# Routed expert layer on one core: fixed row blocks for each expert's first 128 rows, another block order, and twelve constant matmuls behind the ranks

## The chip, the cores and the metric

The program runs on one core of a Trainium2 chip. The metric is the device time of one execution in microseconds. Names of engines: PE is TensorE (PEld its weight loads), DVE is VectorE, ACT is ScalarE, POOL is GpSimd, SP is SyncE, which here only issues DMAs. L12 is line 12 of the kernel.

## The reference

The input x has 1024 rows of 128 values (D). A layer of attention over a context of 6404 rows comes first, then the part that is changed here: a layer of eight experts, of which each row uses one.

```
x = x + cross_attention(layernorm(x), ctx)
xn = layernorm(x)
expert_id = argmax(xn @ wr + br)                 # 8 experts
h = gelu(xn @ w1[e] + b1[e])                     # 128 -> 512
y = h @ w2[e] + b2[e]                            # 512 -> 128
out = x + y of the row's own expert
```

## The kernel before

**Tiles.** The 1024 rows are eight tiles of 128. The attention fills the first 172 us of the span. The last of its tiles is late, so the eighth tile takes no part in the sorting of rows by expert: all eight experts are run over it and a mask keeps the right one. These are the eight **dense** blocks. The other seven tiles (TA = 7) are **sent**: each row goes to a place in a table in HBM, sorted by expert, and the table is read back in 14 blocks of 128 rows (NB), one expert to a block. A block that no row fell into is computed as well. There are 22 blocks in all. `DENSE_AT` names the eight places in the order of 22 at which a dense block stands, `SENT_AT` the other fourteen.

**From the router to the table.** PE computes router scores, DVE takes the best expert of each row as a one-hot table (`oneh`), PE turns that into `rank_psum` (a row's number within its expert) and `count_psum` (rows per expert), L1216 to L1223. DVE then computes where each row goes, in a chain in which every instruction waits for the one ahead of it (`link`): blocks per expert (`nblk`), start of each expert (`sblk`), row position (`pos`), L947 to L957. The expert of each block (`bexp`) follows at L961 to L968. POOL sends the seven tiles with one indirect DMA each (L602). SP waits for all seven (`rows_sent`) and reads the blocks back in four batches of 3, 4, 4 and 3 (`block_rows`, L449), first the normalised rows, then the rest (`rest_landed`).

**Weights.** `wp` holds the weights of all experts, 512 columns to each. Which expert a sent block belongs to is known only at run time, so SP copies its 512 KB from `wp` into a slot of `PT` or `qn` (`fetch`, L444), 14 copies, with two ahead of the wait for `rows_sent`. Dense blocks read `wp` in place.

**A block on the engines.** PE's `up(b)` is 16 matmuls (L1276 to L1279), ACT applies GELU twice (L710, L711), DVE takes the low half (L985), PE's `down(b)` is 9 matmuls (L1290 to L1296), DVE finishes the block in two halves (L995 and L1011 for a sent block, L1001 and L1014 for a dense one). PE issues `up` two blocks ahead of `down`. The eighth tile comes to PE through a transpose at L1227, for which DVE normalises it at L762. Sent rows come to PE through `turn(g)`, the transposes of a batch (L1245), which ACT (L700) and DVE (L977) bring back to SBUF. On PE, `turn(0)` stands just ahead of `up` of the first sent block, and two dense `down`s stand behind that `up`. POOL writes each finished sent block to the output by an indirect DMA (L608); the last dense block's result is written by SP (L476).

Of the kernel before, what the change touches and what calls it, by code (L numbers as in the profile page):

```python
# [30 lines left out]
P = 128  # L31


def build(nc, x, ctxT, w3, b3, wlT, b_l, wr, br, w1, b1, w2, b2, out):
# [47 lines left out]
    with es:  # L82
        def sb(name, shape, dt=F32):
            return es.enter_context(nc.sbuf_tensor(name, shape, dt))

        def sem(name):
            return es.enter_context(nc.semaphore(name))

        tri = sb("tri", [P, E, E])
# [52 lines left out]
        kedge = sb("kedge", [P, E, TA])  # L142
        slot_no = sb("slot_no", [P, NB, E])
# [7 lines left out]
        ints = stageT[:, XRE - NB * E:XRE].bitcast(I32)  # L151
# [17 lines left out]
        more = carve(E * TA).rearrange("p (a b) -> p a b", b=TA)  # L169
        below = carve(E * E).rearrange("p (a b) -> p a b", b=E)  # L170
        rank = carve(TA * E).rearrange("p (a b) -> p a b", b=E)
        cand = carve(T * E).rearrange("p (a b) -> p a b", b=E)
        mask = carve(E)
        chosen = carve(NB // 2, F16)
        past = carve(NB * E).rearrange("p (a b) -> p a b", b=E)
        oneh = carve(TA * E // 2, F16).rearrange("p (a b) -> p a b", b=E)
        nblk, sblk, eblk = carve(E), carve(E), carve(E)
        posf, rmx, bexpf = carve(TA), carve(T), carve(NB)
        pos, bexp = carve(TA, I32), carve(NB, I32)
# [93 lines left out]
        block_w_landed = [sem(f"block_w_landed{k}") for k in range(WSLOTS)]  # L273
# [87 lines left out]
        def block_w(b):  # L361

            k = b % WSLOTS
            return spare[k // (WSLOTS // 2)][:, k % (WSLOTS // 2) * 4 * F:(k % (WSLOTS // 2) + 1) * 4 * F]\
                .rearrange("p (a f) -> p a f", f=F)

        @block.sync
        def _(sp):
# [65 lines left out]
            expert_reg = [sp.alloc_register(f"expert{j}") for j in range(NB)]  # L434
            sp.wait_ge(w_low, T)
            sp.wait_ge(experts_ready, 1)
            sp.reg_load(expert_reg[0:FIRST], bexp[0:1, 0:FIRST])
            ex = [sp.snap(r, min_val=0, max_val=E - 1) for r in expert_reg[0:FIRST]]
# [12 lines left out]

            for b in range(FIRST):
                fetch(b)
            sp.reg_load(expert_reg[FIRST:NB], bexp[0:1, FIRST:NB])
            ex += [sp.snap(r, min_val=0, max_val=E - 1) for r in expert_reg[FIRST:NB]]
# [4 lines left out]
            block_rows(0, D, ROW, rest_landed)  # L460
            fetch(3)
            block_rows(1, D, ROW, rest_landed)
            fetch(4)
            fetch(5)
            block_rows(2, 0, D, rows_landed)
            fetch(6)
            block_rows(2, D, ROW, rest_landed)
            fetch(7)
            fetch(8)
            block_rows(3, 0, D, rows_landed)  # L470
            fetch(9)
            block_rows(3, D, ROW, rest_landed)
            for b in range(10, NB):
                fetch(b)
# [5 lines left out]
        def _(pool):  # L480
# [29 lines left out]
            def numbers(dst, n, pattern, base=0):  # L510
# [4 lines left out]
            numbers(kedge[:, :, :].rearrange("p e k -> p (e k)"), E * TA, [[0, E], [P, TA]])  # L515
            numbers(slot_no[:, :, :].rearrange("p b e -> p (b e)"), NB * E, [[P, NB], [0, E]])
            then(nc.gpsimd.memset(tri[:, :, :], float(P)))
            then(nc.gpsimd.affine_select(out=tri[:, :, :], in_=tri[:, :, :], compare_op=ALU.is_gt, fill=0.0, base=0,
                                         pattern=[[1, E], [-1, E]], channel_multiplier=0))
            then(nc.gpsimd.memset(ones16[:, :], 1.0))  # L520
# [199 lines left out]
        def _(dve):  # L720
# [204 lines left out]
            def best(logits, t0, t1):  # L925
# [23 lines left out]
            link(nc.vector.tensor_reduce(out=nblk[:, :], in_=more[:, :, :], axis=AX.X, op=ALU.add))  # L949
            link(nc.vector.tensor_tensor(below[:, :, :], tri[:, :, :],  # L950
                                         nblk[:, :].unsqueeze(1).broadcast_to([P, E, E]), ALU.mult))
            link(nc.vector.tensor_reduce(out=sblk[:, :], in_=below[:, :, :], axis=AX.X, op=ALU.add))
            link(nc.vector.tensor_tensor(rank[:, :, :], rank_psum.rearrange("p (t e) -> p t e", e=E),
                                         sblk[:, :].unsqueeze(1).broadcast_to([P, TA, E]), ALU.add))
# [6 lines left out]
            link(nc.vector.scalar_tensor_tensor(out=eblk[:, :], in0=nblk[:, :], scalar=float(P), in1=sblk[:, :],  # L961
                                                op0=ALU.mult, op1=ALU.add))
            link(nc.vector.tensor_tensor(past[:, :, :], eblk[:, :].unsqueeze(1).broadcast_to([P, NB, E]),
# [70 lines left out]
        def _(pe):  # L1034
# [190 lines left out]

            pe.wait_ge(x2n_ready, H + 1)
# [21 lines left out]
            def weights(b):  # L1248

                if b in SENT_AT:  # L1250
                    return block_w(SENT_AT.index(b))
                k = DENSE_AT.index(b)
                return wp[:, :, k * F:(k + 1) * F]

            def bias_rows(b):

                if b in SENT_AT:
                    return chosen[:, SENT_AT.index(b):SENT_AT.index(b) + 1].broadcast_to([P, P])
                return pick[:, DENSE_AT.index(b), :]
# [89 lines left out]
```

## Time and profile before

| | |
|---|---|
| time, median of 3 runs | 234.27 us (232.66 to 235.13) |
| the profiled execution's own time | 234.39 us |
| its span, first to last instruction | 232.7 us |
| busy share of the span: PE, DVE, ACT, POOL | 86%, 78%, 68%, 55% |
| mean granted TensorE clock | 0.944 |
| matmuls on PE, instructions on DVE | 1837, 395 |

The shares are means over two stages with different limits, the attention and the experts. The change lies in the second, which begins at about 172 us, so the views below are cut to stretches of time. The granted clock is 1.00 at 2.4 GHz and 0.50 at 1.2 GHz. The span is 1.69 us shorter than the execution's own time.

### The profile page before, as it was taken

What the parts mean: (1) busy time and instruction counts of PE and PEld (TensorE: products, weight loads), DVE (VectorE), ACT (ScalarE), POOL (GpSimd) and SP (SyncE); (2) the same over time, 40 slices, a digit from 0 to 9 for tenths busy, and PEclk for the clock granted to TensorE, in tenths of its full rate; (3) what the DMA queues carried; (4) which work ended last, traced back from release to release, by engine and by line L of the source; (5) the groups of instructions that cost most, each with busy time, mean ns of one, the idle gap of its engine ahead of it and who ended that gap; (6) DMA issues with size and microseconds to landing.
All of it is one profiled execution on the core that took longest, in us unless ns stands there. A gap on an engine that the chain in (4) does not pass through costs nothing.

```text
span 232.7 us, 5011 instructions
## 1 busy us (share of the span) xinstructions
PE 201.1 (86%) x1837; PEld 150.3 (65%) x1837; DVE 180.6 (78%) x395; ACT 157.9 (68%) x249; POOL 128.6 (55%) x177
## 2 busy tenths in 40 slices
PE   0379969999999999989989899899993797999980
PEld 0133417776766767757666566789973686899970
DVE  2899797697998998998995997958756435776872
ACT  2752899399399699699595799689531445667650
POOL 3695718807915807978508947744400740066763
PEclk9999985899999999999999999999996569999998
DMA  6999979899999999999999999988994369999200
GB/s 215 389 251 263 226 223 237 192 234 174 220 215 216 278 230 269 241 198 233 216 213 256 184 220 258 201 196 185 239 263 121 120 219 290 346 370 378 98 11 12
DMA packets 142958, 51.78 MB, mean 223 GB/s; under 512 B 121172, under 2 KB 140773, under 8 KB 142934
## 3 DMA queue, kind: packets, MB, share of 16 engines
q1 hardware_dynamic: 142000, 50.08, 93.2%
q0 software_dynamic: 784, 1.38, 1.7%
q8 instruction: 14, 0.23, 0.4%
q14 instruction: 10, 0.08, 0.1%
q10 hardware_dynamic: 150, 0.00, 0.0%
HBM read 10.74 MB, written 3.75 MB: 62 GB/s over the span
## 4 chain that ended last, share of the span: by engine, by line
PE 49%; DVE 21%; DMA 11%; issue 8%; ACT 4%; POOL 3%; SPq 2%; DVEq 0%; POOLq 0%
DMA PT<-Phl 10%; PE psX L1079 5%; PE psS L1061 5%; PE psO L1079 5%; PE psS L1060 5%; PE psS L1059 5%; DVE S L800 5%; DVE Phl L817 3%; PE psS L1290 3%; PE psX L1081 3%; PE psO L1081 3%; ACT S L651 3%; SPq L393 2%; PE psS L1276 2%; PE psS L1296 2%
## 5 line engine op out<-in xcount | busy, mean ns | idle before, releaser
L651 ACT ACTIVATE S<-S,negb 128x1024 f32<-128x1024 f32 x48 | 55.1, 1147 | 18.4 <-DVE negb L808 18.4
L800 DVE TENSOR_SCALAR_CACHE_REDUCE S<-psS 128x1024 f32<-128x1024 f32 x48 | 58.2, 1217 | 11.4 <-PE psS L1061 11.2
L817 DVE TENSOR_TENSOR Phl<-S,Phl 128x1024 f16<-128x1024 f32 x38 | 51.5, 1355 | 5.0 <-ACT Phl L666 4.8
L533 POOL TENSOR_TENSOR Phl<-S,Phl 128x256 f16<-128x256 f32 x40 | 26.3, 689 | 51.7 <-ACT Phl L666 51.7
L666 ACT CAST Phl<-S 128x1024 f16<-128x1024 f32 x48 | 50.3, 1047 | 5.2 <-DMA PT<-Phl 3.7
L1059 PE MATMUL psS<-qT,gh 128*128 128x512 f16 x96 | 37.7, 393 | 5.4 <-DVE S L800 2.6
L1079 PE MATMUL psX<-qn,PT 128*128 128x256 f16 x204 | 36.4, 273 | 2.1 <-DMA PT<-Phl 2.1
L1079 PE MATMUL psO<-qn,PT 128*128 128x256 f16 x204 | 37.3, 276 | 0.9 <-DMA PT<-Phl 0.8
L1061 PE MATMUL psS<-qT,gl 128*128 128x512 f16 x96 | 37.9, 395 | 0.0
L1060 PE MATMUL psS<-qT,gh 128*128 128x512 f16 x96 | 37.9, 394 | 0.0
L1081 PE MATMUL psO<-qn,PT 128*128 128x128 f16 x204 | 35.7, 221 | 0.0
L1081 PE MATMUL psX<-qn,PT 128*128 128x128 f16 x204 | 35.0, 219 | 0.0
L608 POOL DMA_INDIRECT out_x<-stageT,S x14 | 17.7, 1265 | 22.1 <-DVE stageT L1011 17.1
L1079 PEld LDWEIGHTS psX<-qn,PT 128*128 128x128 f16 x204 | 20.0, 98 | 7.5 <-DMA PT<-Phl 3.5
L1079 PEld LDWEIGHTS psO<-qn,PT 128*128 128x128 f16 x204 | 20.3, 99 | 6.3 <-DMA PT<-Phl 1.9
L710 ACT ACTIVATE Phl<-psS 128x512 f16<-128x512 f32 x22 | 13.2, 598 | 15.4 <-PE psS L1279 9.0
L1081 PEld LDWEIGHTS psO<-qn,PT 128*128 128x128 f16 x204 | 20.2, 99 | 2.2 <-issue 0.3
L1081 PEld LDWEIGHTS psX<-qn,PT 128*128 128x128 f16 x204 | 20.0, 98 | 1.9
L1059 PEld LDWEIGHTS psS<-qT,gh 128*128 128x128 f16 x96 | 9.8, 102 | 14.6 <-DVE S L800 3.5
L1061 PEld LDWEIGHTS psS<-qT,gl 128*128 128x128 f16 x96 | 9.7, 101 | 12.1 <-issue 1.4
L985 DVE TENSOR_TENSOR Phl<-Phl 128x512 f16<-128x512 f32 x22 | 15.0, 682 | 2.4 <-issue 2.4
L574 POOL TENSOR_TENSOR wp<-wp 128x256 f16<-128x256 f32 x16 | 15.6, 1005 | 0.3
(239 smaller groups left out, 425.3 us busy)
## 6 DMA issues: line engine op xcount, KB each, us to landing
PT<-wp SPq DMA_DIRECT2D x8, 512.0 KB, 6.0
stageT<-in_ctxT SPq DMA_DIRECT2D x6, 512.0 KB, 7.0
qn<-wp SPq DMA_DIRECT2D x6, 512.0 KB, 7.3
wp<-in_w SPq DMA_DIRECT2D x4, 512.0 KB, 4.9
stageT<-in_w SPq DMA_DIRECT2D x4, 512.0 KB, 4.9
rows_by_expert<-stageT SPq DMA_DIRECT2D x4, 385.5 KB, 5.6
PT<-Phl SPq DMA_TRANSPOSE x48, 4.2
S<-rows_by_expert SPq DMA_DIRECT2D x2, 258.0 KB, 5.4
```

The costliest lines, as they stand in the source:

```text
L533: last = nc.gpsimd.tensor_tensor(lo[:, r], slot(t, e)[:, r], hi[:, r], ALU.subtract)
L574: last = nc.gpsimd.tensor_tensor(parts[:, 1, at + a:at + a + CHUNK], src[:, a:a + CHUNK], parts[:, 0, at + a:at + a + CHUNK], ALU.subtract)
L608: pool.indirect_dma_start(out=out, out_offset=bass.IndirectOffsetOnAxis(ap=rows[:, b, 2 * D:ROW].bitcast(I32), axis=0), in_=yf[:, b, :], i ...
L651: nc.scalar.activation(slot(t, e), slot(t, e), ACT.Exp, bias=negb[:, t:t + 1], accum_out=Lp[:, t * NG + e:t * NG + e + 1]).then_inc(exp_do ...
L666: nc.scalar.copy(hi, slot(t, e)).then_inc(high_done, 1)
L800: nc.vector.tensor_scalar(out=into, in0=bank(u, n)[:, 0:into.shape[1]], scalar1=1.0 / GS, scalar2=None, op0=ALU.mult, op1=ALU.max, accum_o ...
L817: nc.vector.tensor_tensor(lo, slot(t, e), hi, ALU.subtract).then_inc(low_done, 1)
L1059: nc.tensor.matmul(dst, g_h, hi, start=True, stop=False)
L1060: nc.tensor.matmul(dst, g_h, lo, start=False, stop=False)
L1061: last = nc.tensor.matmul(dst, g_l, hi, start=False, stop=True)
L1079: nc.tensor.matmul(acc[:, 0:2 * D].rearrange("p (a d) -> p a d", a=2), PT[:, 2 * e * TW + i, :], both[:, :, i, :], start=(j == 0), stop=Fa ...
L1081: last = nc.tensor.matmul(acc[:, 0:D], PT[:, 2 * e * TW + n + i, :], both[:, 0, i, :], start=False, stop=(j == QT - 1), skip_group_check=True)
```

## The change

The table of 14 blocks stays, but its blocks have another meaning. Blocks 0 to 7 belong to experts 0 to 7 and take each expert's first 128 rows. Blocks 8 to 13 (NX = 6 of them) take rows past the first 128 of any expert, and only their expert is found at run time. So eight of the fourteen sent blocks read their weights in `wp` in place, with constant bias rows (`pick`), and six are copied by `fetch`. SP issues no copy ahead of `rows_sent` any more.

The position is now computed by expert times 128, plus rank, plus a shift if the rank is 128 or more: two more instructions in the chain on DVE, and a copy of a constant ahead of it. POOL makes one more column of a table of constants (two small instructions in the attention's time). `DENSE_AT` becomes six dense blocks first, fourteen sent, two dense last. PE computes twelve matmuls of 512 columns on constants (`fill`) between the ranks and the transpose at L1227; nothing reads their result.

```diff
-    NB = TA + E - 1
+    NX = TA - 1
+    NB = E + NX
-    DENSE_AT = (0, 1, 2, 3, 4, 10, 16, 21)
+    DENSE_AT = (0, 1, 2, 3, 4, 5, 20, 21)
-    ROUTE_CONSTS = 19
-    WSLOTS = 12
-    FIRST = 2
+    ROUTE_CONSTS = 21
...
-            def fetch(b):
-
-                if b >= WSLOTS:
-                    sp.wait_ge(y_in_psum, SENT_AT[b - WSLOTS] + 1)
-                sp.dma_start(block_w(b), wp[:, :, bass.ds(ex[b] * F, F)]).then_inc(block_w_landed[b % WSLOTS], 16)
+            def fetch(k):
+
+                sp.dma_start(block_w(k), wp[:, :, bass.ds(ex[k] * F, F)]).then_inc(block_w_landed[k], 16)
...
-            for b in range(FIRST):
-                fetch(b)
...
             sp.wait_ge(rows_sent, 16 * TA)
             block_rows(0, 0, D, rows_landed)
             block_rows(1, 0, D, rows_landed)
+            block_rows(0, D, ROW, rest_landed)
+            block_rows(1, D, ROW, rest_landed)
+            block_rows(2, 0, D, rows_landed)
+            fetch(0)
+            block_rows(2, D, ROW, rest_landed)
+            fetch(1)
+            block_rows(3, 0, D, rows_landed)
             fetch(2)
...
-            numbers(slot_no[:, :, :].rearrange("p b e -> p (b e)"), NB * E, [[P, NB], [0, E]])
...
+            numbers(slot_no[:, :, :].rearrange("p b e -> p (b e)"), NX * E, [[P, NX], [-P, E]], base=(E - 1) * P)
...
+            numbers(tri[:, :, E], E, [[-P, E]], base=(E - 1) * P)
...
+            link(nc.vector.tensor_copy(extra[:, E:E + 1], ones[:, 0:1]))
             dve.wait_ge(ranks_in_psum, 1)
-            link(nc.vector.tensor_tensor(more[:, :, :], count_psum.unsqueeze(2).broadcast_to([P, E, TA]),
+            link(nc.vector.tensor_tensor(more[:, :, :], count_psum.unsqueeze(2).broadcast_to([P, E, NX]),
                                          kedge[:, :, :], ALU.is_gt))
...
-            link(nc.vector.tensor_tensor(rank[:, :, :], rank_psum.rearrange("p (t e) -> p t e", e=E),
-                                         sblk[:, :].unsqueeze(1).broadcast_to([P, TA, E]), ALU.add))
+            link(nc.vector.tensor_reduce(out=shift[:, :], in_=below[:, :, :], axis=AX.X, op=ALU.add))
+            ranks = rank_psum.rearrange("p (t e) -> p t e", e=E)
+            link(nc.vector.scalar_tensor_tensor(out=over[:, :, :], in0=ranks, scalar=float(P),
+                                                in1=shift[:, :].unsqueeze(1).broadcast_to([P, TA, E]),
+                                                op0=ALU.is_ge, op1=ALU.mult))
+            link(nc.vector.scalar_tensor_tensor(out=rank[:, :, :], in0=iob.broadcast_to([P, TA, E]), scalar=float(P),
+                                                in1=ranks, op0=ALU.mult, op1=ALU.add))
+            link(nc.vector.tensor_tensor(rank[:, :, :], rank[:, :, :], over[:, :, :], ALU.add))
...
+            filler = ones[:, :].bitcast(F16)
+
+            def fill(n):
+
+                for _ in range(n):
+                    nc.tensor.matmul(psS[2][:, 0:CH], filler[:, 0:P],
+                                     filler.unsqueeze(1).broadcast_to([P, 2, 2 * P]), start=True, stop=True)
+
+            fill(12)
+
             pe.wait_ge(x2n_ready, H + 1)
             nc.tensor.transpose(x7T_psum, x2n[:, TA, :], idf[:, :]).then_inc(x7T_in_psum, 1)
...
             def weights(b):
 
-                if b in SENT_AT:
-                    return block_w(SENT_AT.index(b))
-                k = DENSE_AT.index(b)
-                return wp[:, :, k * F:(k + 1) * F]
+                j = SENT_AT.index(b) if b in SENT_AT else DENSE_AT.index(b)
+                return wp[:, :, j * F:(j + 1) * F] if j < E else block_w(j - E)
...
                     pe.wait_ge(xT_low, g + 1)
-                    pe.wait_ge(block_w_landed[j % WSLOTS], 16 * (j // WSLOTS + 1))
-                    pe.wait_ge(chosen_rows, 1)
+                    if j >= E:
+                        pe.wait_ge(block_w_landed[j - E], 16)
+                        pe.wait_ge(chosen_rows, 1)
```

The order of instructions is written out by hand, so the diff moves them at three places. The first is DVE's chain from the ranks to the positions. Before (S holds the small tables of the router; kedge and tri are tables of constants):

```order
L737 BN_AGGR mv<-st 128x2 [waits dve_chain]
L947 TENSOR_TENSOR S<-psS,kedge 128x56 [waits ranks_in_psum,dve_chain]
L949 TENSOR_REDUCE S<-S 128x8 [waits dve_chain]
L950 TENSOR_TENSOR S<-tri,S 128x64 [waits dve_chain]
L952 TENSOR_REDUCE S<-S 128x8 [waits dve_chain]
L953 TENSOR_TENSOR S<-psS,S 128x56 [waits dve_chain]
L955 TENSOR_TENSOR S<-S 128x56 [waits dve_chain]
L956 TENSOR_REDUCE S<-S 128x7 [waits dve_chain]
L957 CAST S<-S 128x7 [waits dve_chain]
```

Now, the same place on DVE:

```order
L726 BN_AGGR mv<-st 128x2 [waits dve_chain]
L935 COPY S<-ones 128x1 [waits dve_chain]
L937 TENSOR_TENSOR S<-psS,kedge 128x48 [waits ranks_in_psum,dve_chain]
L939 TENSOR_REDUCE S<-S 128x8 [waits dve_chain]
L940 TENSOR_TENSOR S<-tri,S 128x72 [waits dve_chain]
L942 TENSOR_REDUCE S<-S 128x8 [waits dve_chain]
L944 SCALAR_TENSOR_TENSOR S<-psS,S 128x56 [waits dve_chain]
L947 SCALAR_TENSOR_TENSOR S<-iota_e,psS 128x56 [waits dve_chain]
L949 TENSOR_TENSOR S<-S 128x56 [waits dve_chain]
L950 TENSOR_TENSOR S<-S 128x56 [waits dve_chain]
L951 TENSOR_REDUCE S<-S 128x7 [waits dve_chain]
L952 CAST S<-S 128x7 [waits dve_chain]
```

The copy and two instructions on 128x56 are new; the rest of the chain is as long as it was.

The second place is PE between the ranks and the first dense block. Before:

```order
L1223 MATMUL psS<-S,ones 128x8 x7
L1227 MATMUL psO<-idf,qT 128x128 [waits x2n_ready]
L1276 MATMUL psS<-S,wp 128x128 [waits w_low,x7T_low,route_consts,b12_ready]
L1277 MATMUL psS<-S,wp 128x128
L1278 MATMUL psS<-S,wp 128x128
```

Now, on PE:

```order
L1218 MATMUL psS<-S,ones 128x8 x7
L1226 MATMUL psS<-ones 128x512 x12
L1232 MATMUL psO<-idf,qT 128x128 [waits x2n_ready]
L1279 MATMUL psS<-S,wp 128x128 [waits w_low,x7T_low,route_consts,b12_ready]
L1280 MATMUL psS<-S,wp 128x128
```

The twelve matmuls wait for nothing but stand ahead of the transpose of the eighth tile.

The third place is SP's queue behind the filling of the empty table (ISA is a register instruction ahead of a copy). Before:

```order
L437 TENSOR_LOAD S [waits experts_ready,w_low]
L438 ISA
L444 DMA PT<-wp 128x4x512
L444 ISA
L444 DMA PT<-wp 128x4x512
L454 TENSOR_LOAD S
L455 ISA x2
L449 DMA S<-rows_by_expert 128x3x128 [waits rows_sent]
L449 DMA S<-rows_by_expert 128x4x128
L444 ISA
L444 DMA PT<-wp 128x4x512
L449 DMA S<-rows_by_expert 128x3x129
```

Now, on SP:

```order
L436 TENSOR_LOAD S [waits experts_ready,w_low]
L437 ISA
L446 DMA S<-rows_by_expert 128x3x128 [waits rows_sent]
L446 DMA S<-rows_by_expert 128x4x128
L446 DMA S<-rows_by_expert 128x3x129
L446 DMA S<-rows_by_expert 128x4x129
L446 DMA S<-rows_by_expert 128x4x128
L441 ISA
L441 DMA PT<-wp 128x4x512
```

The two copies of weights that stood ahead of the row reads are gone, and five row reads stand ahead of the first copy.

## Rows read from the trace of the kernel before

**Rows 1.** Stretches: us, busy of PE, PEld, DVE, ACT, POOL, granted clock, DMA share, GB/s.

```profile
182.40:189.00 6.60, 6.60 (x55) 6.25 (x56) 1.99 (x10) 2.32 (x5) 5.08 (x6) 0.50 0.69 245
189.00:190.00 1.00, 1.00 (x12) 0.88 (x11) 0.00 (x0) 0.00 (x0) 0.47 (x1) 0.68 0.26 95
...
193.60:195.43 1.83, 0.56 (x4) 0.32 (x4) 1.73 (x4) 1.13 (x3) 0.00 (x0) 1.00 1.05 344
...
195.43:227.63 32.20, 30.91 (x454) 29.07 (x454) 21.60 (x57) 20.20 (x38) 16.33 (x13) 1.00 0.72 240
```

**Rows 2.** PE in order of time, 176 to 196 us: start, us, line, idle before.

```profile
176.96 0.33 PE L1223 MATMUL psS<-S,ones 128*128 128x8 f16 x7
181.07 0.48 PE L1227 MATMUL psO<-idf,qT 128*128 128x128 f32 x1 [3.78 <-DVE qT L762]
182.39 0.27 PE L1276 MATMUL psS<-S,wp 128*128 128x128 f16 x1 [0.84 <-DVE S L966]
...
185.16 0.27 PE L1276 MATMUL psS<-S,wp 128*128 128x128 f16 x1
...
193.72 0.55 PE L1245 MATMUL psX<-idf,S 128*128 128x128 f32 x3
195.43 0.23 PE L1276 MATMUL psS<-S,PT 128*128 128x128 f16 x1 [1.16 <-DVE S L977]
```

**Rows 3.** DVE in order of time, 177 to 229 us.

```profile
177.44 0.22 DVE L947 TENSOR_TENSOR S<-psS,kedge 128x56 f32<-128x56 f32 x1
...
179.20 0.17 DVE L957 CAST S<-S 128x7 int32<-128x7 f32 x1
...
180.67 0.35 DVE L762 TENSOR_SCALAR qT<-qT,mv,rstd 128x128 f32<-128x128 f32 x1
...
185.41 0.69 DVE L985 TENSOR_TENSOR Phl<-Phl 128x512 f16<-128x512 f32 x1 [2.38 <-issue]
...
225.71 0.28 DVE L1011 TENSOR_TENSOR stageT<-psS,stageT 128x128 f32<-128x128 f32 x1
...
228.12 0.35 DVE L1014 SCALAR_TENSOR_TENSOR stageT<-psS,S,stageT 128x128 f32<-128x128 f32 x1
```

**Rows 4.** POOL in order of time, 35 to 229 us.

```profile
35.66 2.56 POOL L533 TENSOR_TENSOR Phl<-S,Phl 128x256 f16<-128x256 f32 x4 [5.58 <-ACT Phl L666]
...
185.60 1.33 POOL L602 DMA_INDIRECT rows_by_expert<-qT,S  x1 [0.30 <-issue]
187.24 0.96 POOL L602 DMA_INDIRECT rows_by_expert<-qT,S  x1 [0.30 <-issue]
...
228.33 0.98 POOL L608 DMA_INDIRECT out_x<-stageT,S  x1 [0.31 <-issue]
```

**Rows 5.** SP's DMA issues in order of time, 183 to 192 us.

```profile
183.90 1.50 SPq L444 DMA_DIRECT2D PT<-wp  x2
191.11 0.90 SPq L449 DMA_DIRECT2D S<-rows_by_expert  x2
```

**Rows 6.** PE in order of time, 201 to 204 us, two sent blocks.

```profile
201.39 0.23 PE L1276 MATMUL psS<-S,PT 128*128 128x128 f16 x1 [0.30 <-DVE S L977]
...
203.01 0.22 PE L1276 MATMUL psS<-S,PT 128*128 128x128 f16 x1
...
203.90 0.60 PE L1290 MATMUL psS<-PT,Phl 128*128 128x256 f16 x4
```

**Rows 7.** All waits of PE from 195 us: us in total, times, longest.

```profile
PE psS L1276 <- DVE S L977: 1.5, 2, 1.2
PE psS L1296 <- DVE Phl L985: 1.0, 2, 0.5
```

**Rows 8.** PE in order of time, 32 to 35 us, behind a pause in the attention.

```profile
32.37 0.39 PE L1059 MATMUL psS<-qT,gh 128*128 128x512 f16 x1 [2.27 <-DVE S L800]
...
33.40 0.63 PE L1059 MATMUL psS<-qT,gh 128*128 128x512 f16 x1
...
34.26 0.63 PE L1061 MATMUL psS<-qT,gl 128*128 128x512 f16 x1
```

More of the change, by code:

```diff
@@ L87, in sem @@
             return es.enter_context(nc.semaphore(name))
-        tri = sb("tri", [P, E, E])
+        tri = sb("tri", [P, E, E + 1])
         mv = sb("mv", [P, T, 2])
@@ L141, in build @@
         iota_e = sb("iota_e", [P, E])
-        kedge = sb("kedge", [P, E, TA])
-        slot_no = sb("slot_no", [P, NB, E])
+        kedge = sb("kedge", [P, E, NX])
+        slot_no = sb("slot_no", [P, NX, E])
         row_no = sb("row_no", [P, 1])
@@ L166, in build @@
         rows = carve(NB * ROW).rearrange("p (b w) -> p b w", w=ROW)
-        more = carve(E * TA).rearrange("p (a b) -> p a b", b=TA)
-        below = carve(E * E).rearrange("p (a b) -> p a b", b=E)
+        more = carve(E * NX).rearrange("p (a b) -> p a b", b=NX)
+        below = carve(E * (E + 1)).rearrange("p (a b) -> p a b", b=E + 1)
         rank = carve(TA * E).rearrange("p (a b) -> p a b", b=E)
+        over = carve(TA * E).rearrange("p (a b) -> p a b", b=E)
         cand = carve(T * E).rearrange("p (a b) -> p a b", b=E)
         mask = carve(E)
-        chosen = carve(NB // 2, F16)
-        past = carve(NB * E).rearrange("p (a b) -> p a b", b=E)
+        chosen = carve(NX // 2, F16)
+        past = carve(NX * E).rearrange("p (a b) -> p a b", b=E)
         oneh = carve(TA * E // 2, F16).rearrange("p (a b) -> p a b", b=E)
-        nblk, sblk, eblk = carve(E), carve(E), carve(E)
-        posf, rmx, bexpf = carve(TA), carve(T), carve(NB)
-        pos, bexp = carve(TA, I32), carve(NB, I32)
+        extra, shift, eblk = carve(E + 1), carve(E), carve(E)
+        posf, rmx, bexpf = carve(TA), carve(T), carve(NX)
+        pos, bexp = carve(TA, I32), carve(NX, I32)
         parts_ring = Phl[:, :, :, :].rearrange("p r a w -> p (r a w)")
@@ L272, in build @@
         rest_landed = [sem(f"rest_landed{g}") for g in range(len(BATCHES))]
-        block_w_landed = [sem(f"block_w_landed{k}") for k in range(WSLOTS)]
+        block_w_landed = [sem(f"block_w_landed{k}") for k in range(NX)]
         chosen_rows = sem("chosen_rows")
@@ L359, in piece, with block_w @@
                     PT[:, 2 * e * TW:2 * e * TW + 2 * n, :])
[L361 to L365, printed above, removed]
+        def block_w(k):
+            half = (NX + 1) // 2
+            return spare[k // half][:, k % half * 4 * F:(k % half + 1) * 4 * F].rearrange("p (a f) -> p a f", f=F)
         @block.sync
@@ L432, in _ @@
                              empty[:, :].unsqueeze(1).broadcast_to([P, k1 - k0, ROW])).then_inc(slots_emptied, 16)
-            expert_reg = [sp.alloc_register(f"expert{j}") for j in range(NB)]
+            expert_reg = [sp.alloc_register(f"expert{j}") for j in range(NX)]
             sp.wait_ge(w_low, T)
             sp.wait_ge(experts_ready, 1)
-            sp.reg_load(expert_reg[0:FIRST], bexp[0:1, 0:FIRST])
-            ex = [sp.snap(r, min_val=0, max_val=E - 1) for r in expert_reg[0:FIRST]]
-            def fetch(b):
-                if b >= WSLOTS:
-                    sp.wait_ge(y_in_psum, SENT_AT[b - WSLOTS] + 1)
-                sp.dma_start(block_w(b), wp[:, :, bass.ds(ex[b] * F, F)]).then_inc(block_w_landed[b % WSLOTS], 16)
+            sp.reg_load(expert_reg[0:NX], bexp[0:1, 0:NX])
+            ex = [sp.snap(r, min_val=0, max_val=E - 1) for r in expert_reg]
+            def fetch(k):
+                sp.dma_start(block_w(k), wp[:, :, bass.ds(ex[k] * F, F)]).then_inc(block_w_landed[k], 16)
             def block_rows(g, a, b, done):
@@ L458, in _ @@
             block_rows(1, 0, D, rows_landed)
-            fetch(2)
[L460 to L471, printed above, removed]
+            block_rows(0, D, ROW, rest_landed)
[5 more added lines that the diff above has]
+            block_rows(3, 0, D, rows_landed)
+            fetch(2)
             block_rows(3, D, ROW, rest_landed)
-            for b in range(10, NB):
-                fetch(b)
+            for k in range(3, NX):
+                fetch(k)
             sp.wait_ge(y_ready, DENSE_AT[E - 1] + 1)
@@ L514, in _ @@
             numbers(iota_e[:, :], E, [[1, E]])
-            numbers(kedge[:, :, :].rearrange("p e k -> p (e k)"), E * TA, [[0, E], [P, TA]])
-            numbers(slot_no[:, :, :].rearrange("p b e -> p (b e)"), NB * E, [[P, NB], [0, E]])
-            then(nc.gpsimd.memset(tri[:, :, :], float(P)))
-            then(nc.gpsimd.affine_select(out=tri[:, :, :], in_=tri[:, :, :], compare_op=ALU.is_gt, fill=0.0, base=0,
+            numbers(kedge[:, :, :].rearrange("p e k -> p (e k)"), E * NX, [[0, E], [P, NX]], base=P)
+            numbers(slot_no[:, :, :].rearrange("p b e -> p (b e)"), NX * E, [[P, NX], [-P, E]], base=(E - 1) * P)
+            then(nc.gpsimd.memset(tri[:, :, 0:E], float(P)))
+            then(nc.gpsimd.affine_select(out=tri[:, :, 0:E], in_=tri[:, :, 0:E], compare_op=ALU.is_gt, fill=0.0, base=0,
                                          pattern=[[1, E], [-1, E]], channel_multiplier=0))
+            numbers(tri[:, :, E], E, [[-P, E]], base=(E - 1) * P)
             then(nc.gpsimd.memset(ones16[:, :], 1.0))
```

18 lines of the change are left out of this document (7 added, 11 removed).

## The prediction

> **What bounds the kernel now.** I read the stretches of the expert stage first, because the shares of the whole span mix it with the attention. From 195.43 us on, PE is busy for 30.91 of 32.20 us at a granted clock of 1.00 [rows 1]: the sent blocks are PE's. Ahead of that it is another story. From 182.40 to 189 us PE is busy all the time, but at a clock of 0.50, which is 1.2 GHz, and between 193.60 and 195.43 us it is busy for 0.56 us only [rows 1].
>
> PE in order of time says why. The ranks end at 176.96 + 0.33 = 177.29 us, then PE idles 3.78 us until DVE has normalised the eighth tile, transposes it at 181.07, and starts the first dense block at 182.39. At 193.72 the first batch of sent rows is transposed, and the first sent block starts at 195.43, behind 1.16 us of idle time that ended with DVE's low half of those rows [rows 2]. So the dense blocks are cover, and the first sent block waits for the rows. Their chain starts with the ranks: DVE computes positions from 177.44 to 179.20 + 0.17 = 179.37 us [rows 3], POOL sends seven tiles, SP sees them landed and reads the first batch at 191.11 [rows 5], PE transposes it at 193.72 [rows 2]. From 179.37 to 195.43 it is 16.06 us, on POOL, DMA and the round trip PE, ACT, DVE.
>
> Two things therefore set the end: when the first sent block can start, and how much PE work is left then.
>
> **The change, part by part.**
>
> *Positions.* From L947 to the cast, seven steps take 179.20 - 177.44 = 1.76 us, 0.25 each [rows 3]. The two new instructions work on 128x56, as their neighbours do: +0.50. The new copy of one column stands ahead of the wait for the ranks, which came at 177.29, before L947 started at 177.44 [rows 2, 3], so nothing hides it: +0.20, with 0 and 0.25 as its bounds. Positions are 0.70 us late.
>
> *Rows.* The number of scatters and the first two reads are what they were, so I keep the 16.06 us. The first sent block starts at 195.43 + 0.70 = 196.13 us, its transposes at 193.72 + 0.70 = 194.42. The two copies of 512 KB that SP issued at 183.90 [rows 5] no longer run beside the scatters. I give nothing for that, since POOL issues the scatters one behind the other; at best it is 0.37, by which one of them was longer (1.33 against 0.96) [rows 4].
>
> *One dense block more in front.* A block takes PE 203.01 - 201.39 = 1.62 us, of which `up` is 203.90 - 203.01 = 0.89 and `down` 0.73 [rows 6]. The first sent `up` now has one `up` and one `down` fewer behind it. PE's end is 196.13 + 32.20 - 1.62 = 226.71 us against 227.63: **0.92 us earlier**. That is the whole gain. What PE saves ahead of the first sent block only makes it wait there.
>
> *Fill.* The twelve matmuls start at 177.29 us. The clock is low there, and at the low clock two matmuls of 512 columns start 34.26 - 33.40 = 0.86 us apart [rows 8], so twelve take 12 x 0.43 = 5.16 us, until 182.45; at the full clock half of that, until 179.9. The eighth tile is ready at 180.67 + 0.35 + 0.70 = 181.72 us [rows 3], so in the worse case the fill holds its transpose until 182.45, 1.38 later than the 181.07 of before. The first dense block then starts at 182.39 + 1.38 = 183.77. Six `up` and four `down` are 6 x 0.89 + 4 x 0.73 = 8.26 us; between the first `up` and the second stand the router's matmuls for the eighth tile, at most 185.16 - 182.39 - 2 x 0.89 = 1.0 us [rows 2]. At the full clock PE is through at 193.0, which leaves 1.4 us of cover before 194.42. So the fill and the sixth dense block cost nothing if the clock is back by then. If it comes back as late as before, at 189.64 (0.68 is the mean of 189 to 190 us [rows 1]), PE is through at about 195.5, which is 1.1 late.
>
> *Weights.* Eight copies of 512 KB go, and six stay, behind the reads of rows. From 195 us PE waits only for DVE, never for a copy [rows 7], so this is worth nothing. The first copy is needed eight sent blocks, 13 us, after the first of them starts.
>
> *The end.* The last sent block becomes block 19 of 0 to 21. Block 19's result was ready at 225.71 + 0.28 = 225.99 us [rows 3], which is now 0.92 earlier, 225.1. POOL's last issue, for block 20, stood at 228.33 to 229.31 [rows 4]; it now comes a block's time earlier and ends by 228 us even if POOL lags. The last dense result is ready at 228.12 + 0.35 - 0.92 = 227.55 [rows 3], with its write behind it, so the end follows that result: the 0.92 goes through whole, and no more than that.
>
> *Tables.* Two small instructions more on POOL lie ahead of a pause of 5.58 us that ended with ACT [rows 4]; if that cover were gone they would cost some 0.3 us.
>
> Sum: 234.39 - 0.92 = **233.5 us**, against the profiled execution; the median of before, 234.27, is 0.12 under it, so the change is 0.3%.
>
> **The rivals.**
>
> *A. The clock falls in the wait ahead of the sent blocks (slower side).* With the clock back early, PE is idle from 193.0 to 194.42, does 0.55 us of transposes, and idles again until 196.13: 2.6 us of idle time where it had some 1.3 [rows 1, 2]. In the attention a pause of 2.27 us [rows 8] was followed by the low clock (0.43 us per 512 columns at 33.40); the shorter one at 193.60 was not (1.00 [rows 1]). The new pause is nearer to the long one. After the second `up` started at 185.16 [rows 2], PE worked 4.48 us before the clock returned at 189.64. The same here costs half of it, 2.24, less the 0.30 us stall at 201.39 [rows 6], which the slower PE would fill: 1.9 us. PE then ends at 226.71 + 1.9, and the time is 235.4. It decides from a low stretch of 1.84 us on, which eats the 0.92. The Trainium skill, "TensorE: Matmul & The Clock Gate", section "HAM oscillation — how this bites in real kernels", says that matmul bursts with waits for data between them get throttled again and start each burst cold. By that rule the six dense blocks are one burst and the sent blocks the next, and the fill, which warms the first, would lengthen the wait before the second; the trace agrees at 33.40 us and not at 193.60.
>
> *B. More scatters collide with DVE.* The scatter at 185.60 took 1.33 us while L985 ran from 185.41 to 186.10; one without such company took 0.96 [rows 3, 4]. With a faster PE three or four L985 fall among the seven scatters instead of one. Two more collisions make 0.74 us, and the time 234.2. The Trainium skill, "SBUF — State Buffer", section "SBUF: two separate sides", says that a DMA issued from GpSimd cannot write its descriptors while DVE holds the port pair they share. That would make it 186.10 - 185.60 = 0.50 us for this scatter; measured is 0.37.
>
> *C. The fill doesn't bring the clock back.* Then the dense blocks run as slowly as before from a later start: `up` at half clock from 183.77, the second `up` at 186.6, the clock back 4.48 us later at 191.1, and 5.1 of 8.26 us of work left: through at 196.2, 1.8 after the rows. The time is 233.5 + 1.8 = 235.3. For it speaks that the small matmuls of the router and the ranks did not keep the clock; against it that twelve matmuls of 512 columns leave no gap.
>
> *D. The rows come sooner.* If the copy is hidden (0.20) and no scatter is held up (0.37), the first sent block starts at 195.56 and the time is 232.9. To be faster by over 1% the rows would have to land about 0.7 us earlier than before, though their chain is longer; only the copies that no longer run beside the scatters speak for that.
>
> **How the numbers follow.** Forecast 0.36; A 0.28; B 0.12; C 0.11; D 0.13. Predicted time: that of the forecast, 233.5. A measurement of this kernel tells 1% from no change, here 2.34 us: under 231.9 is faster, over 236.6 slower. No case has its own time beyond these bounds. Faster needs the far end of D, with the copies' traffic worth over 1 us, or a gain of that size on top of the forecast: 0.14. Slower needs a low clock of over 6.5 us in A, or A and C together: 0.12. The range takes in A and C with 0.5 us of spread above them and D with 0.9 below it: 232.0 to 235.9.
>
> **What would show it.** In the profile after: the cast of positions 0.7 us later behind the ranks; 12 matmuls 0.43 us apart, or 0.22 if the clock is up; the granted clock at 1.00 from about 184 us; the last dense `up` done by 193; the first sent block at 196.1 with over 2 us of idle time ahead of it; PE's end 30.6 us after that. The clock in the 5 us after the first sent block tells the forecast from A, the dense `up` in front of the first transposes B from C: a PE that idles there was held by the rows, one that works there by its clock. The prediction is wrong if the first sent block starts before 195.4, or if PE's end doesn't follow it by 30.6 us at the full clock.

## The result, and the profile after

The changed kernel takes **250.17 us** (median of 4 runs, 250.06 to 251.7) against 234.63 us for the kernel before on the same chip (4 runs). The ratio is 1.0701, 95% interval 1.0634 to 1.0768. The forecast was 233.5 us within 232.0 to 235.9, with 0.12 on slower, so it was wrong by 16.7 us. The profiled execution took 250.06 us, 15.67 us longer than the one of before, with a span of 248.3 us. In what follows times are medians of all runs of a kernel and ratios leave out its slow runs, of which one, of the kernel 64 bytes off, took 352.0 us at a granted clock of 0.576.

The first question is where the time went. From the page of the kernel before, a line on the DMA queue that carries the most, the chain of waits by engine, two groups of instructions (busy, mean ns | idle time ahead of them, releaser), and a DMA group with its median time to landing:

```profile
q1 hardware_dynamic: 142000, 50.08, 93.2%
...
PE 49%; DVE 21%; DMA 11%; issue 8%; ACT 4%; POOL 3%; SPq 2%; DVEq 0%; POOLq 0%
...
L666 ACT CAST Phl<-S 128x1024 f16<-128x1024 f32 x48 | 50.3, 1047 | 5.2 <-DMA PT<-Phl 3.7
...
L1079 PE MATMUL psX<-qn,PT 128*128 128x256 f16 x204 | 36.4, 273 | 2.1 <-DMA PT<-Phl 2.1
...
PT<-Phl SPq DMA_TRANSPOSE x48, 4.2
```

The same lines of the page after:

```profile
q1 hardware_dynamic: 137776, 45.89, 91.5%
...
PE 35%; DMA 27%; DVE 19%; issue 6%; SPq 6%; ACT 4%; another core or an unknown queue 2%; DVEq 0%; ACTq 0%
...
L655 ACT CAST Phl<-S 128x1024 f16<-128x1024 f32 x48 | 50.2, 1045 | 25.9 <-DMA PT<-Phl 24.9
...
L1074 PE MATMUL psX<-qn,PT 128*128 128x256 f16 x204 | 38.0, 279 | 11.5 <-DMA PT<-Phl 11.4
...
PT<-Phl SPq DMA_TRANSPOSE x48, 5.1
```

All of this is the attention, which the diff does not touch. ACT's cast works as long as before (50.2 us), but it waits 24.9 us in place of 3.7 for the DMA transposes of Phl into PT, which free the part of Phl it wants to fill. PE waits 11.4 us for them in place of 2.1. A transpose lands 5.1 us after its issue, not 4.2. DMA's share of the chain goes from 11% to 27%. The queue moves 4.19 MB less and is busy longer: 93.2% of 232.7 us is 216.9 us, 91.5% of 248.3 is 227.2.

PE in order of time after, 192 to 214 us, answers to [rows 2]:

```profile
192.61 0.33 PE L1218 MATMUL psS<-S,ones 128*128 128x8 f16 x7
192.79 5.28 PE L1226 MATMUL psS<-ones 128*128 128x512 f16 x12
197.87 0.42 PE L1232 MATMUL psO<-idf,qT 128*128 128x128 f32 x1
199.13 0.22 PE L1279 MATMUL psS<-S,wp 128*128 128x128 f16 x1 [0.84 <-DVE S L961]
...
203.74 0.23 PE L1299 MATMUL psS<-wp,Phl 128*128 128x128 f16 x1 [0.47 <-issue]
204.46 0.22 PE L1279 MATMUL psS<-S,wp 128*128 128x128 f16 x1 [0.49 <-issue]
205.17 0.22 PE L1280 MATMUL psS<-S,wp 128*128 128x128 f16 x1 [0.49 <-issue]
...
205.88 0.22 PE L1282 MATMUL psS<-stageT 128*128 128x128 f16 x1 [0.43 <-issue]
206.58 0.22 PE L1279 MATMUL psS<-S,wp 128*128 128x128 f16 x1 [0.49 <-issue]
...
211.93 0.50 PE L1250 MATMUL psX<-idf,S 128*128 128x128 f32 x3
213.87 0.23 PE L1279 MATMUL psS<-S,wp 128*128 128x128 f16 x1 [1.44 <-DVE S L972]
```

The ranks end at 192.61 + 0.33 = 192.94 us, where they ended at 177.29 [rows 2]: **15.65 us late, the whole loss**. From there to the end of the span it is 248.3 - 192.94 = 55.36 us, against 232.7 - 177.29 = 55.41 before. So the stage that the prediction argued about came out even, and the stage that it took as given lost everything. Five pauses inside the dense blocks, in which PE waited for nothing that the profile shows, are new as well; they come back below.

### The profile page after: what moved, and what is told of

Same layout as the page of the kernel before. It is cut to its first block, busy times and chain, and to the rows that moved or that the text cites. A ratio compares the mean times of both kernels' runs of the same rounds, so it can differ in the third digit from the quotient of the medians.

```text
span 248.3 us, 5014 instructions
## 1 busy us (share of the span) xinstructions
PE 202.6 (82%) x1849; PEld 146.2 (59%) x1849; DVE 179.9 (72%) x398; ACT 157.6 (63%) x249; POOL 125.9 (51%) x179
## 3 DMA queue, kind: packets, MB, share of 16 engines
q1 hardware_dynamic: 137776, 45.89, 91.5%
## 4 chain that ended last, share of the span: by engine, by line
PE 35%; DMA 27%; DVE 19%; issue 6%; SPq 6%; ACT 4%; another core or an unknown queue 2%; DVEq 0%; ACTq 0%
DMA PT<-Phl 25%; DVE S L789 6%; SPq L392 5%; PE psX L1074 5%; DVE Phl L806 3%; PE psS L1293 3%; PE psS L1054 2%; ACT Phl L655 2%; PE psS L1056 2%; PE psS L1055 2%; PE psX L1076 2%; PE psS L1226 2%; PE psS L1299 2%; PE psS L1282 2%
## 5 line engine op out<-in xcount | busy, mean ns | idle before, releaser
L655 ACT CAST Phl<-S 128x1024 f16<-128x1024 f32 x48 | 50.2, 1045 | 25.9 <-DMA PT<-Phl 24.9
L806 DVE TENSOR_TENSOR Phl<-S,Phl 128x1024 f16<-128x1024 f32 x38 | 50.2, 1322 | 17.4 <-ACT Phl L655 17.2
L1074 PE MATMUL psX<-qn,PT 128*128 128x256 f16 x204 | 38.0, 279 | 11.5 <-DMA PT<-Phl 11.4
L1074 PE MATMUL psO<-qn,PT 128*128 128x256 f16 x204 | 36.8, 273 | 8.9 <-DMA PT<-Phl 8.7
L1054 PE MATMUL psS<-qT,gh 128*128 128x512 f16 x96 | 37.2, 387 | 4.5 <-DVE gl L767 3.0
L1055 PE MATMUL psS<-qT,gh 128*128 128x512 f16 x96 | 37.1, 387 | 0.0
L1056 PE MATMUL psS<-qT,gl 128*128 128x512 f16 x96 | 37.0, 385 | 0.0
L1076 PE MATMUL psX<-qn,PT 128*128 128x128 f16 x204 | 36.4, 223 | 0.0
L1076 PE MATMUL psO<-qn,PT 128*128 128x128 f16 x204 | 35.2, 219 | 0.0
L1074 PEld LDWEIGHTS psX<-qn,PT 128*128 128x128 f16 x204 | 20.4, 100 | 20.0 <-DMA PT<-Phl 16.2
L1074 PEld LDWEIGHTS psO<-qn,PT 128*128 128x128 f16 x204 | 19.9, 98 | 16.3 <-DMA PT<-Phl 13.0
L1076 PEld LDWEIGHTS psX<-qn,PT 128*128 128x128 f16 x204 | 20.4, 100 | 1.4
L1076 PEld LDWEIGHTS psO<-qn,PT 128*128 128x128 f16 x204 | 20.0, 98 | 1.4
L1279 PE MATMUL psS<-S,wp 128*128 128x128 f16 x64 | 14.0, 219 | 3.6 <-DVE S L972 1.7
```

The costliest lines, as they stand in the source:

```text
L655: nc.scalar.copy(hi, slot(t, e)).then_inc(high_done, 1)
L806: nc.vector.tensor_tensor(lo, slot(t, e), hi, ALU.subtract).then_inc(low_done, 1)
L1054: nc.tensor.matmul(dst, g_h, hi, start=True, stop=False)
L1055: nc.tensor.matmul(dst, g_h, lo, start=False, stop=False)
L1056: last = nc.tensor.matmul(dst, g_l, hi, start=False, stop=True)
L1074: nc.tensor.matmul(acc[:, 0:2 * D].rearrange("p (a d) -> p a d", a=2), PT[:, 2 * e * TW + i, :], both[:, :, i, :], start=(j == 0), stop=Fa ...
```

## Why the attention: the start of one tensor

The diff makes the table `tri` wider, from 8x8 to 8x9 numbers (a line that the diff ahead of the prediction leaves out): 256 bytes of each partition become 288. `tri` is the first tensor of SBUF that the kernel allocates, and the tensors follow one another in the order of their lines. So every large tensor behind it starts 32 bytes later: Phl at byte 134,688 in place of 134,656, which is 526 x 256. **Theory:** the DMA transposes are slower from or to the shifted starts, and nothing else of the change costs anything like this. **Rival:** something in the new code of the expert stage (the fill, the moved blocks, the fewer copies) reaches back into the attention. The first four runs tell them apart.

**The shift alone.** The kernel before, with 32 unused bytes ahead of the table:

```diff
+        pad = sb("pad", [P, 8])
         tri = sb("tri", [P, E, E])
```

> The kernel before with nothing changed but an unused tensor of 32 bytes per partition ahead of the first one, so that every tensor behind it starts 32 bytes higher, as the wider table does it in the change. Address theory (the attention's DMA transposes are slower between tensors that no longer start on a multiple of 512 bytes, or of 64): about 250 us, the ranks at about 193 us of the span. Rival (the two new table instructions on POOL, or anything else in the changed program's order, upsets the attention): 234.5 us, ranks at 177.

Measured: 251.82 us, ratio 1.0733 (1.0658 to 1.0808). None of the change is in it, and the whole loss is there.

**The change without the shift.** The wider table goes behind the last tensor, and three small tensors of 256 bytes together take its place:

```diff
-        tri = sb("tri", [P, E, E + 1])
+        st = sb("st", [P, T, 6])
+        mx = sb("mx", [P, T])
+        negb = sb("negb", [P, T])
...
         token = sb("token", [P, T], I32)
+        tri = sb("tri", [P, E, E + 1])
```

> The changed kernel with the table of constants moved behind the last tensor and three small tensors of 256 bytes in all in its place, so that the large tensors have the addresses of the kernel before. All new instructions stay. Address theory: ranks at about 177 us again, and the time 234.5 plus or minus 1 (in the changed kernel the stretch from the ranks to the end was as long as before, 55.5 against 55.4 us). Rival (order): 250 us.

Measured: 234.17 us, ratio 0.9984 (0.9947 to 1.0021). The rival falls: all of the new code is in this kernel, and nothing is lost. I call it the aligned kernel from here on.

**64 bytes.** The changed kernel with `pad` of 32 bytes ahead of its table, so 64 above the old starts:

> The changed kernel with 32 bytes more ahead, so that the large tensors start 64 bytes above a multiple of 512. Address theory with a grain of 64 bytes: 234.5 us. With a grain of 512 bytes: about 250 us. Order rival: 250 us.

Measured: 249.95 us, ratio 1.0642 (1.0555 to 1.0729). The grain is coarser than 64 bytes.

**No fill.** The aligned kernel with `fill(0)` for `fill(12)`:

> As a_aligned, without the twelve constant matmuls. If the fill only warms a stretch that has cover (my forecast's view), the first sent block starts when the rows are there, and the time is that of a_aligned within 0.5 us, or some 1 to 1.5 less if a PE that runs the dense blocks at half clock no longer pauses and so keeps its clock. If the fill is needed (rival C's price), it is 1 to 2 us slower than a_aligned.

Measured: 232.2 us, ratio 0.9909 (0.9879 to 0.9939), 2.0 us under the aligned kernel, where at most 1.5 was expected. Its reading comes with the pauses below.

**Which tensor, which grain.** In the kernel before, `sc2` (32 bytes) was moved ahead of Phl and 480 bytes of small tensors ahead of PT, so that only Phl and its tail shift; or `sc2` ahead of PT and the 480 bytes behind it, so that only PT does:

```diff
+        sc2 = sb("sc2", [P, T])
         Phl = sb("Phl", [P, PARTS, 2, GR], F16)
         Ptail = sb("Ptail", [P, 2, TAILP], F16)
+        st = sb("st", [P, T, 6])
+        Lp = sb("Lp", [P, T * NG])
+        mx = sb("mx", [P, T])
+        negb = sb("negb", [P, T])
         PT = sb("PT", [P, 2 * QT, P], F16)
```

> The kernel before with only Phl and its tail Ptail, from which the transposes of the attention read, 32 bytes above a multiple of 512; PT, to which they write, and all other large tensors still start on a multiple. If the start of what is read decides, this is as slow as the kernel before with everything shifted: 249 to 252 us. If the start of what is written decides, 234 to 235 us. If both count, in between (238 to 246 us).

> The kernel before with only PT, to which the transposes of the attention write, 32 bytes above a multiple of 512; Phl and all other large tensors start on a multiple. If the start of what is written decides, 249 to 252 us. If the start of what is read decides, 234 to 235 us. If both count, this loss and that of the kernel with only Phl moved add up to about 15.5 us.

Measured: 250.06 us with only Phl shifted, ratio 1.065 (1.0593 to 1.0707), and 234.94 us with only PT shifted, ratio 1.0048 (0.9998 to 1.0097). Of the pages of these two kernels, first Phl's, then PT's, the lines of ACT's cast and of the transposes:

```profile
L666 ACT CAST Phl<-S 128x1024 f16<-128x1024 f32 x48 | 50.3, 1047 | 21.9 <-DMA PT<-Phl 20.8
...
PT<-Phl SPq DMA_TRANSPOSE x48, 5.1
```

```profile
L666 ACT CAST Phl<-S 128x1024 f16<-128x1024 f32 x48 | 50.2, 1047 | 4.6 <-DMA PT<-Phl 3.1
...
PT<-Phl SPq DMA_TRANSPOSE x48, 4.2
```

It is the start of what the transposes **read**, and not of what they write; the small tensors that were moved are the same five in both kernels, so it isn't they. Then the grain, in the changed kernel with small tensors moved ahead of its table (`mx`, `negb`, `sc2` for 96 bytes; `st`, `negb` for 224):

> The changed kernel with 96 bytes of small tensors moved ahead of the table, so that the large tensors start 128 bytes above a multiple of 512. If the grain that matters is 128 bytes, about 234 us, as with the large tensors on a multiple of 512; if it is 256 or 512, about 250 us.

> The changed kernel with 224 bytes of small tensors moved ahead of the table, so that the large tensors start 256 bytes above a multiple of 512. If the grain is 256 bytes, the length of one packet of these transposes, about 234 us; if it is 512, about 250 us.

Measured: 250.61 us at 128 bytes, ratio 1.0674 (1.0611 to 1.0737), and 233.93 us at 256, ratio 0.9963 (0.9907 to 1.002). At 256 bytes the cast hardly waits:

```profile
L655 ACT CAST Phl<-S 128x1024 f16<-128x1024 f32 x48 | 50.3, 1047 | 7.0 <-DMA PT<-Phl 5.7
...
PT<-Phl SPq DMA_TRANSPOSE x48, 4.2
```

So the source has to start on a multiple of 256 bytes, and 32, 64 and 128 bytes off cost the same within their intervals. The trace's packet records show where the time appears. The transposes from Phl, from its tail and, early in the kernel, from qT make the same 117,504 packets of 256 bytes in each kernel. They take 20.7 ns each on average before, 23.5 after, 22.7 with only Phl shifted, 20.3 with only PT shifted and 20.6 at 256 bytes off. The kernel with only Phl shifted has both kinds side by side: the first 13,056 packets, those from qT, which was not moved, take 19.1 ns as before (19.0), and the rest 23.1 (20.9 before). The middle packet stays at 18 ns; what grows is the share that takes 19 ns and more, from 2.5% to 16%. Over 16 engines the sum is 151.9 us before and 172.4 after, 20.5 more, while the ranks end 15.65 later.

The Trainium skill, "DMA: Bandwidth & Descriptors", section "How a descriptor splits into AXI transactions", says that a read has to begin at an address aligned to 256 bytes, so that a descriptor that doesn't start there begins with a transaction from the boundary below. By that rule a row of 256 bytes takes two transactions in place of one from any unaligned start. The trace agrees in the side (the read's) and in the grain of 256. It does not agree with the page's count of beats as the price: an estimate from its examples is 9, 10 and 12 beats for 8 at 32, 64 and 128 bytes, and the times are 250.17, 249.95 and 250.61 us. Nor do the runs show why 84% of the packets take no longer than 18 ns when the rule would hold for all of them.

## The pauses in the dense blocks

With the tensors aligned the change neither gains nor loses, and without the fill it gains 0.9% (0.6 to 1.2%). The stretches after, 199 us to PE's end, answer to [rows 1] (us, busy of PE, PEld, DVE, ACT, POOL, granted clock, DMA share, GB/s):

```profile
199.12:203.28 4.16, 4.15 (x60) 3.81 (x60) 1.71 (x8) 1.25 (x3) 2.97 (x4) 1.00 0.26 95
203.28:206.58 3.30, 0.94 (x5) 0.38 (x6) 0.22 (x2) 0.00 (x0) 1.83 (x2) 1.00 0.34 120
206.58:211.93 5.35, 4.80 (x71) 4.41 (x71) 3.73 (x9) 4.13 (x8) 0.00 (x0) 1.00 0.67 175
...
213.87:244.58 30.71, 29.09 (x429) 27.47 (x429) 20.46 (x54) 18.94 (x36) 16.93 (x14) 1.00 0.43 130
```

The fill does what it is for: the clock is at 1.00 (2.4 GHz) over the dense blocks, where it stood at 0.50 before [rows 1]. But in 203.28 to 206.58 us PE does 0.94 us of work in 3.30. It runs for 60 matmuls, then stops five times, and the clock stays at 1.00. POOL's scatters of the same time, which answer to [rows 4], and SP's read of the rows, which answers to [rows 5]:

```profile
203.19 0.96 POOL L591 DMA_INDIRECT rows_by_expert<-qT,S  x1 [0.30 <-issue]
204.46 0.96 POOL L591 DMA_INDIRECT rows_by_expert<-qT,S  x1 [0.30 <-issue]
```

```profile
206.91 3.56 SPq L446 DMA_DIRECT2D S<-rows_by_expert  x5
```

The pauses stand beside the last scatters. Two theories: the scatters' traffic makes them, or PE runs out of instructions at a fixed place of its stream. Two kernels, both aligned:

```diff
             pool.wait_ge(pos_ready, 1)
+            pool.wait_ge(y_in_psum, 4)
             for t in range(TA):
```

> The changed kernel with the small tensors arranged so that the large ones start on a multiple of 512, and POOL waiting for the fourth dense block's down before it issues the seven scatters, so that the first dense blocks run with no scatter beside them. In the aligned kernel PE paused five times for 0.4 to 0.8 us inside the dense blocks, 5.1 us after the first dense up began. If the scatters' traffic makes those pauses, none stands in the first four blocks, and some appear once the scatters start. If PE's own supply of instructions runs dry at full clock after so many matmuls, they stay 5 us after the first dense up. The time itself says little: the rows come later, so 235 to 240 us by either.

```diff
-            fill(12)
+            fill(24)
```

> The aligned changed kernel with 24 constant matmuls in place of 12. If the pauses inside the dense blocks hang on the scatters, they stand at the same time behind the ranks as with 12, so earlier in the count of dense matmuls. If they hang on how many instructions PE has run since the attention, or on how long the dense blocks have run, they move with the blocks. The longer fill ends behind the x2 transpose's input and delays the dense blocks by 1 to 3 us; the time is 234 to 237 us.

Measured: 243.89 us with late scatters and 233.66 us with 24 matmuls, one run each. The first is more than was expected, since PE idles 13.85 us for the rows there; the second is just under it. The stretch of the dense blocks with late scatters, and POOL's first scatter there:

```profile
180.10:189.15 9.05, 9.03 (x136) 8.56 (x136) 5.54 (x18) 5.48 (x11) 0.00 (x0) 1.00 0.01 2
```

```profile
190.06 1.21 POOL L592 DMA_INDIRECT rows_by_expert<-qT,S  x1 [21.68 <-PE psS L1300]
```

All 136 matmuls run through in 9.05 us at the full clock, without a pause. With 24 matmuls in the fill, the stretch up to the first pause, and the pauses:

```profile
184.00:187.50 3.50, 3.49 (x52) 3.26 (x53) 1.25 (x6) 1.25 (x3) 2.85 (x3) 1.00 0.31 113
```

```profile
187.68 0.27 PE L1293 MATMUL psS<-wp,Phl 128*128 128x256 f16 x1 [0.18 <-issue]
188.40 0.38 PE L1293 MATMUL psS<-wp,Phl 128*128 128x256 f16 x2 [0.45 <-issue]
...
189.81 0.28 PE L1293 MATMUL psS<-wp,Phl 128*128 128x256 f16 x1 [1.03 <-issue]
```

Here the pauses begin after 52 dense matmuls. With 12 in the fill they begin after 60 (the kernel after), 63 (aligned) and 64 (each of those 64, 128 and 256 bytes off). Twelve more in the fill, some twelve fewer behind it: the place in PE's stream is the same within four matmuls, 72 to 76 behind the ranks with 12 and 24 + 52 = 76 with 24. The time is not: the first pause begins 11.3 us behind the ranks with 24, and 10.0 to 10.4 with 12. So each theory holds half. The pauses begin at a fixed place of PE's stream, and they need scatters beside them.

The packets say when they end. Two more stretches of the kernel after, the last pauses and what follows:

```profile
205.88:206.58 0.70, 0.21 (x1) 0.10 (x1) 0.00 (x0) 0.00 (x0) 0.00 (x0) 1.00 0.53 188
206.58:207.40 0.82, 0.82 (x14) 0.77 (x14) 0.35 (x1) 0.79 (x2) 0.00 (x0) 1.00 0.00 0
```

All the traffic of the first stretch is the seventh scatter's. Its last packet ends at 206.51 us, and PE runs on from 206.58. In all six kernels with pauses the last pause ends within 0.1 us of the last scatter's packets (191.32 for 191.31 us in the aligned one, 189.81 for 189.82 with 24). What holds PE up at that place is not shown. That its stream's own transfers (14 packets on the instruction queue q8 of each page) are held up by the scatters would give both, and the eleventh of them speaks for it: with late scatters it starts 0.55 us after PE's 76th matmul, at 184.81, in the aligned kernel 2.87 us after it, at 191.31. But in the kernel after and in that with 24, PE runs on 1.0 and 1.2 us before this packet starts, so the link stays open.

This also explains why the fill is no gain: a PE that comes sooner to that place waits there for the scatters. At the full clock with pauses PE takes from 199.13 to 211.93 us, 12.80 us, for its dense blocks. In the kernel without a fill it takes as long at a mean clock of 0.68, with no pause:

```profile
181.08:193.70 12.62, 12.61 (x136) 12.01 (x137) 5.66 (x18) 5.49 (x11) 5.57 (x6) 0.68 0.42 127
```

Two more runs, both aligned: six matmuls in the fill, and no fill with `DENSE_AT = (0, 1, 2, 3, 4, 10, 20, 21)`, which puts the sixth dense block back among the sent ones.

> The aligned changed kernel with 6 constant matmuls. With 12 it took 234.2 us and paused five times in the dense blocks; with none it took 232.2 us and did not pause, the clock being at 0.50 until 189 us. If the clock's return is what causes the pauses, and 6 matmuls bring it back as 12 do, 234 us; if 6 don't bring it back ahead of the dense blocks, 232.2 us as with none. A time well below 232 would say that half a fill pays.

> The aligned changed kernel without constant matmuls and with the sixth dense block put back from place 5 to place 10, so five dense blocks stand first. By the prediction's sum the sixth dense block in front is worth 0.92 us, work that PE does while it would else wait for rows: then 233.1 us. If PE at half clock is what sets the first sent block (it had no idle time ahead of it with six), five blocks let it start some 1 us sooner and the end stays: 232.2 us.

Measured: 231.9 us with six matmuls, ratio 0.9895 (0.9825 to 0.9966); 232.82 us with five dense blocks in front, ratio 0.9935 (0.9895 to 0.9975), which overlaps that of six in front without a fill, 0.9909 (0.9879 to 0.9939). So half a fill is as good as none: its clock had fallen back to 0.50 from 182 to 188 us, and it had none of the long pauses. That does not show that a slow PE is safe from them. With six matmuls PE comes to its 76th behind the ranks at 188.5 us, with none at 189.7, and POOL has issued its last scatter by then (187.59 and 188.17), whose packets end at 188.69 and 189.27. With six, 0.11 us of idle time do stand there, from 188.68 on. On the five blocks the times decide nothing; the traces, one execution of each kernel, say more. PE in order of time, the ranks and the first sent block, without fill and six dense blocks in front, then with five:

```profile
174.92 0.32 PE L1218 MATMUL psS<-S,ones 128*128 128x8 f16 x7
...
195.65 0.23 PE L1279 MATMUL psS<-S,wp 128*128 128x128 f16 x1 [1.44 <-DVE S L972]
```

```profile
174.41 0.33 PE L1218 MATMUL psS<-S,ones 128*128 128x8 f16 x7
...
193.39 0.23 PE L1279 MATMUL psS<-S,wp 128*128 128x128 f16 x1 [1.16 <-DVE S L972]
```

With six the first sent block starts 195.65 - 175.24 = 20.41 us behind the ranks, with five 193.39 - 174.74 = 18.65. Behind it, to the end of the span, it is 230.1 - 195.65 = 34.45 and 229.2 - 193.39 = 35.81. In these two executions the sixth block saves 1.36 us behind and costs 1.76 in front.

## Why the prediction was wrong

**The step that failed is *Tables*.** It priced the wider table by the two small instructions that fill it, at nothing or 0.3 us, and not by the 32 bytes that it adds ahead of every large tensor. With it fell an assumption that stood in every sum and was not listed as a step: that the ranks end at 177.29 us as before. No rival held this, since all four lay behind the ranks. What the runs showed in its place: these bytes put the ranks 15.65 us later, the start of Phl (with its tail) alone makes the kernel before 6.5% slower, and the change takes 234.17 us once the starts are mended. That is inside the range, but, as the steps below show, not for the forecast's reasons.

Behind the ranks, by the prediction's own steps:

- *Positions*, +0.70: right. The cast answers to [rows 3]; it ends 195.71 - 192.94 = 2.77 us behind the ranks, where it was 179.37 - 177.29 = 2.08, so +0.69.

```profile
195.54 0.17 DVE L952 CAST S<-S 128x7 int32<-128x7 f32 x1
```

- *Rows*: SP's read of the first batch comes 206.91 - 195.71 = 11.20 us after the positions, 0.54 sooner than the 191.11 - 179.37 = 11.74 of before. But it took 3.7 us to land, and 2.6 before (the read after, then that of before):

```profile
S<-rows_by_expert SPq DMA_DIRECT2D x1, 192.0 KB, 3.7
```

```profile
S<-rows_by_expert SPq DMA_DIRECT2D x1, 192.0 KB, 2.6
```

  So the rows were there at 210.6 us, 17.7 behind the ranks, 0.5 later than the 194.42 - 177.29 = 17.13 at which the forecast had PE transpose them. Nor were they what the first sent block waited for in the end: PE came to their transposes at 211.93, another 1.3 us later, with no idle time ahead of it.
- *One dense block more in front* was mis-sized, by its cover. The prediction had PE through with 1.4 us to spare. At the full clock the work is what was worked out, 9.05 us without pauses for 193.0 - 183.77 = 9.23, but with the pauses it takes 12.80. The first sent block starts 213.87 - 192.94 = 20.93 us behind the ranks, 2.09 after the 18.84 of the forecast: 1.86 until PE comes to the transposes, of which the rows alone would have cost 0.5, and 0.23 from there.
- PE's end, 30.58 us behind the first sent block: right, 244.18 + 0.40 - 213.87 = 30.71.
- *Fill*, 12 x 0.43 = 5.16 us: right, 5.28 by its row. The clock is back over the dense blocks (rival C is wrong), and what that buys is spent in the pauses.
- *The end*: the 0.92 was to go through "whole, and no more than that". The chain of waits of before ends on POOL, not on the last dense result:

```profile
227.44 0.90 issue
228.33 0.98 POOL out_x L608
```

and that of after ends on the dense result:

```profile
244.61 0.36 DVE stageT L996
245.07 0.35 DVE stageT L1009
```

From PE's end to the end of the span it was 232.7 - 227.63 = 5.07 us, and is 248.3 - 244.58 = 3.72. Having the last sent block, and with it POOL's last scatter, one block further from the end was worth 1.35 us that the prediction left out.

The sum closes: -0.92 forecast, +2.09 ahead of the first sent block, +0.13 in the sent blocks, -1.35 at the end is -0.05, the 55.36 against 55.41 us. Two errors of opposite sign cancelled, so the even result behind the ranks is luck, and no sign that the forecast understood it.

Of the rivals, B is wrong: none of the seven scatters took 1.33 us after, as one had [rows 4]. A did not occur in the kernel after, whose clock stayed at 1.00 from 199 us to PE's end; in the aligned kernel the clock was at 0.52 from 192.80 to 195.90 us, behind the pauses. D is wrong: the read of the rows was issued 0.54 us sooner, but they landed later than the forecast had them.

## What to carry to other kernels

Before pricing a diff's instructions, price its bytes: a tensor that grows ahead of others moves the start of all of them, and where a stage is paced by DMA transposes the start of what they read is worth more than a moved block. Keep such sources on multiples of 256 bytes, put tables of odd size last, and look in a new profile at the untouched stages first. A clock that comes back sooner pays only if PE then really runs: read the stretch matmul by matmul before counting on it.

## What the runs showed of the hardware that was not expected

- A DMA transpose in SBUF is slower from a source that starts off a multiple of 256 bytes: packets of 256 bytes take 23.3 to 23.5 ns on average with all tensors 32, 64 and 128 bytes off, against 20.3 to 21.0 with the source on a multiple, and 5.0 to 5.1 us to landing against 4.2 to 4.3. The start of the destination made no difference (4.2 us).
- PE pauses three to five times, for 0.2 to 1.1 us, from nearly the same place of its stream on (72 to 76 matmuls behind the ranks) if POOL's indirect scatters run beside it. In six of six such kernels it runs on within 0.1 us of the end of the last scatter's packets. In the one run with the scatters later it passes that place without a pause. Whether the clock matters for it is open: no kernel came to that place at half the clock while scatters were being issued.
